# Audio tower on one core: large transfers behind the store of the attended heads, two norms at the start of their units

## What is computed

```python
h = _L0_tok_ref(x, W, b, gamma, beta)          # einsum, norm over 256, gelu
h = h + _L0_attn_ref(_layernorm(h), Wq, bq, Wk, bk, Wv, bv, Wo, bo)
h = h + _L0_ffn_ref(_layernorm(h), ...)        # 0 tokens picked: a norm with ln_g, ln_b is left

# _L0_attn_ref
Q, K, V = (proj(Wq, bq), proj(Wk, bk), proj(Wv, bv))
scores = einsum('bhqd,bhkd->bhqk', Q, K) / sqrt(16)
out = einsum('bhqk,bhkd->bhqd', softmax(scores, axis=-1), V)
return out @ Wo.T + bo
```

## Time and profile before

| | |
|---|---|
| median of 3 runs | 2451.26 us (2450.72 to 2453.55) |
| profiled execution, its own time | 2454.76 us |
| its span in the trace | 2453.0 us |
| PE, ACT busy | 91%, 88% |
| DVE, POOL busy | 38%, 15% |
| mean granted clock of PE | 0.972 |
| ACT idle before L494 | 133.9 us |
| ACT idle before L486 (start of the kernel) | 80.4 us |

### The profile page before, as it was taken

How to read it: one execution, slowest core, us unless ns; L and a number is a source line. 1 busy time by engine, 2 the same in 40 slices (tenths; PEclk the granted TensorE clock), 3 DMA queues, 4 the chain that set the end, 5 groups by cost and what they waited for, 6 DMA issues and landing times.

```text
span 2453.0 us, 75572 instructions
## 1 busy us (share of the span) xinstructions
PE 2220.3 (91%) x33324; PEld 613.4 (25%) x33324; DVE 920.1 (38%) x2075; ACT 2153.5 (88%) x2332; POOL 370.5 (15%) x495
## 2 busy tenths in 40 slices
PE   4589999999999999999999999999999999988892
PEld 1222222222222222222222222222222222222221
DVE  7442235532354234533345233542335332330114
ACT  0098999989999899998999899998999989999991
POOL 2211002211021111210112110211112111110002
PEclk7799999999999999999999999999999999999996
DMA  2311221222112222212212221222222122111101
GB/s 71 107 38 40 60 74 41 58 66 67 45 47 67 64 69 49 59 49 59 74 42 51 73 63 45 51 59 64 70 55 51 42 66 69 47 45 39 34 7 32
DMA packets 110030, 135.39 MB, mean 55 GB/s; under 512 B 32263, under 2 KB 89670, under 8 KB 109694
## 3 DMA queue, kind: packets, MB, share of 16 engines
q1 hardware_dynamic: 107158, 128.64, 20.9%
q10 hardware_dynamic: 2536, 1.83, 0.3%
HBM read 55.16 MB, written 61.44 MB: 48 GB/s over the span
## 4 chain that ended last, share of the span: by engine, by line
issue 49%; PE 21%; ACT 14%; POOL 8%; DVE 3%; DMA 2%; POOLq 1%; SPq 1%; DVEq 0%; ACTq 0%
PE PS L856 9%; ACT prob L489 6%; PE PS L830 6%; ACT prob L486 5%; PE PS L790 4%; POOL sq L380 2%; POOL Y L388 2%; ACT prob L494 2%; POOL rs L390 2%; DMA qk_halves_scratch<-HL 1%; SPq L246 1%; DVE HL L568 1%; DVE HL L566 1%; POOLq L389 1%; DVE z L550 1%
## 5 line engine op out<-in xcount | busy, mean ns | idle before, releaser
L856 PE MATMUL PS<-prob,Vst 125*32 125x500 f32 x9216 | 1131.2, 593 | 0.2 <-ACT prob L489 0.2
L494 ACT ACTIVATE prob<-PS 125x1000 f32<-125x1000 f32 x768 | 776.7, 1011 | 133.9 <-PE PS L830 131.8
L486 ACT ACTIVATE prob<-PS 125x1000 f32<-125x1000 f32 x768 | 776.4, 1011 | 80.4 <-PE PS L830 80.4
L830 PE MATMUL PS<-QA,KA 64*32 64x500 f16 (+1 forms) x18432 | 751.9, 381 | 97.5 <-ACT prob L489 48.8
L489 ACT ACTIVATE prob<-PS 125x1000 f32<-125x1000 f32 x768 | 786.7, 1024 | 0.0
L830 PEld LDWEIGHTS PS<-QA,KA 64*32 64x32 f16 (+1 forms) x18432 | 200.5, 90 | 907.3 <-ACT prob L486 416.2
L856 PEld LDWEIGHTS PS<-prob,Vst 125*32 125x32 f32 x9216 | 218.7, 108 | 431.2 <-issue 241.7
L566 DVE TENSOR_SCALAR HL<-PS,b_qk 128x500 f16<-128x500 f32 x96 | 70.9, 738 | 502.9 <-PE PS L790 426.8
L790 PE MATMUL PS<-zT,w_qk 128*32 128x500 f32 x1536 | 197.4, 596 | 9.0 <-DVE Osb L611 7.5
L380 POOL TENSOR_TENSOR sq<-HL 128x2000 bf16<-128x2000 f16 x24 | 84.5, 3520 | 751.4 <-DVE HL L568 751.4
L611 DVE COPY Osb<-PS 128x500 f32<-128x500 f32 x96 | 64.9, 677 | 256.7 <-PE PS L856 256.7
(11 more groups left out here) (79 smaller groups left out, 961.5 us busy)
## 6 DMA issues: line engine op xcount, KB each, us to landing
qk_halves_scratch<-HL SPq DMA_DIRECT2D x384, 125.0 KB
QA<-qk_halves_scratch SPq DMA_DIRECT2D x64, 375.0 KB, 5.2
KA<-qk_halves_scratch SPq DMA_DIRECT2D x64, 375.0 KB, 7.4
oT<-On SPq DMA_DIRECT2D x384, 31.2 KB, 2.0
out<-Y SPq DMA_DIRECT2D x24, 500.0 KB
X<-in_x SPq DMA_DIRECT2D x8, 468.8 KB, 8.0
thin<-Osb SPq DMA_DIRECT2D x96, 7.8 KB
Den<-thin SPq DMA_DIRECT2D x96, 7.8 KB
```

The source lines that it names most:

```text
L486: act.activation(prob[0:T, 6 * p:6 * p + 2, :], PS[0:T, 0:2, 0:QC], ACT.Exp, scale=scl)\
L494: act.activation(prob[0:T, 6 * p + 4:6 * p + 6, :], PS[0:T, 4:6, 0:QC], ACT.Exp, scale=scl)\
L830: last = pe.matmul(PS[lo:hi, bank, 0:QC], KA[rows, G % 2, h // 2, t * T + lo:t * T + hi], QA[rows, G % 2, h // 2, c * QC:(c + 1) * QC], st ...
L856: last = pe.matmul(PS[lo:lo + 2 * HD, 6 + n % 2, 0:QC], Vst[:, b % 2, t, g * HG + j, :], prob[0:T, (HG * t + j) % 12, :], start=(t == 0), ...
```

## The change

The change does two things. In `NORMS` the second norm of chunk 1 goes from (4,4) to (4,0), and that of chunk 2 from (6,6) to (6,0); that of chunk 0 stays at (2,3). On SP the stores of finished output and the load of the next waveform go from the start of their unit to r = 5, behind `store_attended`; the store of chunk 1 goes from unit 1 to unit 2, where it stands behind the load. `load_group` goes to the same place, which for it is the same order as before, since no transfer stood between. Lines behind the SP block have numbers greater by one in the changed kernel.

```diff
-    NORMS = {(2, 3): 0, (4, 4): 1, (6, 6): 2}
+    NORMS = {(2, 3): 0, (4, 0): 1, (6, 0): 2}
...
                     if n > 0:
                         spread_sums(n - 1)
-                    if u in (0, 1, 3) and b > 0:
-                        store_out(b - 1, min(u, 2))
-                    if u == 2 and b + 2 < B:
-                        load_x(b + 2)
                     for r in range(PER):
                         for what, pb, i, last in pieces(b, u, r):
...
                         if r == 5 and n > 0:
                             store_attended(n - 1)
-                    if u % NC == 1 and n + 2 < B * NU:
-                        load_group(n // NC + 1)
+                        if r == 5:
+                            if u == 2 and b + 2 < B:
+                                load_x(b + 2)
+                            if u in (0, 2, 3) and b > 0:
+                                store_out(b - 1, max(0, u - 1))
+                            if u % NC == 1 and n + 2 < B * NU:
+                                load_group(n // NC + 1)
```

## The result

The changed kernel takes 2413.77 us (median of 4, 2412.07 to 2414.54) where the kernel before takes 2450.99 (median of 4, 2450.59 to 2453.55; the three of them that stood on record before gave 2451.26): a ratio of 0.9845, 95% interval 0.9828 to 0.9862. The forecast was 2411 in a range of 2403 to 2424. In the profiled executions the span goes from 2453.0 to 2412.7 us, by 40.3; the sum of the prediction was 40.4.

A forecast was written before the change was run, and what follows sets the result against it. ACT (88% busy) and PE (91%) were taken to bound the kernel; two stalls of ACT, 32.2 and 8.2 us, come off: 2454.8 to 2414.4 us profiled, 2451.3 - 40.4 = 2410.9 us by medians, range 2403 to 2424.

The forecast's parts named there:

- the sum of the prediction: Whole kernel: idle ACT time to be won in units 4 and 6, 32.2 and 8.2 us, together 40.4 us.
- the two stalls: PE waits for DVE behind norms at (4,4) and (6,6), seven times each; ACT loses 32.2 and 8.2 us.
- a second cost: End of unit 4: after PE's 2.98 us wait its granted clock falls to 0.55, so ACT loses more.
- The room on DVE: Start of units 4 and 6: DVE idle 7.71 and 7.50 us, norm 4.75, leaving 2.9 and 2.7 before the take.
- The product `On`: Unit 4: about 0.3 us overlap with POOL's squares, ending at 814.1 where they end at 813.6; no matmul delayed.
- The squares: Unit 4: POOL's squares, 3.52 us, hold the norm's root at (4,4); norm 6.5 us there, 4.75 at (4,0).
- The transfers: Large stores and load on SP issued at r = 5: gain 0, upper end 1.6 us, cost 0.
- The margin: Unit 4: spread of the sums lands half a microsecond before DVE's inversion, behind which DVE is idle 4 us more.
- One stall left: Rival: one stall stays or returns elsewhere, such as unit 6's 8.2 us; 2419 us, chance 0.04.
- PE's own waits alone are given back: Rival: only PE's waits, 28.4 us, return, as ACT's idle time reappears in PE-bound periods; 2423 us, chance 0.05.
- the block of `On`: Rival: squares hold `On`, wait moves to value tile 3; at most 2.4 us in 7 batches, 2428 us, chance 0.03.
- The slower case: Rival: store delays the spread some 10 us past the inversion's turn in unit 4; 2455 to 2465 us, chance 0.02.

The follow-up runs named there:

- unit 4 alone: Kernel before with only the norm of chunk 1 moved to (4,0), transfers as before: 2421.45 us, ratio 0.9868.
- the second 41.7: The changed kernel measured once more, nothing edited, beside the kernel before: 2412.77 us against 2454.49, ratio 0.9837.
- the kernel with unit 6 alone: Kernel before with only the norm of chunk 2 moved to (6,0), transfers as before: 2441.84 us, ratio 0.9953.
- the experiment with the root ahead: Kernel before, norm kept at (4,4); POOL does its root before the squares of chunk 0, bias sum behind both: 2469.98 us, ratio 1.0065.
- A doubled store: Changed kernel with one spare 500 KB store behind each store of finished output of batches 0 to 6: 2413.00 us, ratio 0.9831 to the kernel before.
- a tripled one: Changed kernel with two spare stores behind each output store of batches 0 to 6: 2453.88 us, ratio 0.9997 to the kernel before.
- the kernel with the squares last: Kernel before, norm kept at (4,4); POOL does root, bias sum and only then the squares of chunk 0: 2431.04 us, ratio 0.9909.

## Why the prediction was right

**The bound and the two stalls.** That ACT loses 4 to 5.6 us at the end of unit 4 and 1.18 us in unit 7 in seven batches was read rightly. With both norms moved the span is 40.3 us shorter (40.4 in the sum), and each part gives about its term: 32.6 us for unit 4 alone (32.2), and 7.7 to 8.3 us for unit 6 on top of it (8.2).

**The size against the medians.** The first comparison gave 37.2 us, the second 41.7. The sum against the profiled execution, 2414.4, was nearer to the result (2413.8 and 2412.8) than the forecast of 2410.9 made from it. The step that was off is the move from that execution to the median: it took 3.5 us off both kernels alike, because "the stalls are in every batch alike". The stalls are, but what the clock adds to them is not: it differs between batches of one execution, as the kernel with unit 6 alone shows, and the kernel before spreads over 7 us where the changed one spreads over 2.5. So a low execution of the kernel before has, as far as the runs tell, smaller stalls and less to win, and says little of the changed one. I named the clock as a second cost, but took it as fixed; the range should have had a reason from it, and had none.

**The room on DVE.** In unit 4 2.9 us were forecast between norm and take, 3.01 measured; in unit 6 of batch 3 it was 2.7, and 2.83 measured. The product `On` was to end 0.5 us behind the squares and hold no one: 0.54, and no wait.

**The squares.** The prediction took the norm to cost 6.5 us at (4,4) and 4.75 elsewhere. That was right, but I had treated POOL's work only as something that holds its root and the product. That it also holds the write of `z` was missed, and only the experiment with the root ahead showed it; it did not touch the forecast, since at (4,0) and (6,0) POOL has no such work beside `z`.

**The transfers.** Forecast 0, measured 0 in both directions: the norms alone are as fast as the whole, the transfers alone as slow as before. The margin was put at 0.5 us and then 4 of idle DVE. It was 1.7 at most. A doubled store costs nothing and a tripled one 41 us; I had put the point at which all the gain is lost at a landing some 10 us behind the inversion's turn, and with DVE waiting 11.07 us there the gain was lost to within the measurement.

**The rivals.** One stall left would have been 2419; the kernel that leaves the one of unit 6 has 2421.5. That PE's own waits alone are given back (2423) is refuted by both medians. It was also the time by the sentence of the Trainium skill, page "TensorE: Matmul & The Clock Gate", section "Loop structure matters more than you think", on copies by DVE; but the page draws that with matmuls that follow at once, and here PE stood 2.98 us for DVE's take. What I called the block of `On` does not occur here, but its kin in the experiment with the root ahead made the kernel 15 us slower than before instead of 25 faster. The slower case exists and lies beyond a doubling of what the change moves.

## What to carry to other kernels

Ask of every helper step that an in-order engine does between two takes of a shared bank: what does it wait for on the other engine, what is queued ahead there, and what runs there while it works. The cure is a stretch in which both engines are free, not just an earlier one; moving POOL's step alone made it worse by 15 us before it made it better by 23. A wait of PE of some 3 us cost ACT 3.0 us where the clock stayed up and 4.1 to 5.6 where it fell, so cost it with both ends. Of moved transfers, look for the small one that now stands behind them and for the time until someone wants it.

## What the runs showed of the hardware

- The same idle time of PE, 2.98 us with the same work on both sides, was followed by a clock of 1.00 in two batches and of 0.50 to 0.56 for two microseconds in the others of the same execution; the 1.27 us of the kernel with the squares last were followed by a clock of 1.00 in all seven batches, and 4.47 us cost ACT 5.55 us and more in every batch.
- Four small writes of `z` by DVE (tensor_scalar, float32 from SBUF to SBUF) took 1.38 us alone and 4.57 us when POOL's product of 3.52 us starts 0.07 us before them, while the statistics of the norm took as long beside POOL's squares as without them: 1.39 us in the earlier trace rows with POOL idle, and in unit 4 before, with the squares of the earlier trace rows running from 810.08 on:

```profile
809.92 1.40 DVE L541 BATCH_NORM_STATS2 st<-Hs 125x6 f32<-125x256 f32 x4
```

- The spread of the sums, 7.8 KB, landed later the more SP had issued ahead of it: behind 0.5 MB of stores DVE did not wait for it in unit 4 of batch 3, behind 1.5 MB it stood 11.07 us.
